# The order of ScalarE's work in one outer-layer step, and one pass for x plus normed x

## The reference, cut to what matters

```
xn   = layernorm(x)                                   # 6250 x 256
agg  = [sum, max, mean of the edge rows by target node]       # 3 x 96
x1   = x + (relu([xn, agg, u0] @ W1 + b1) @ W2 + b2 + xn)     # hidden 1024
x2   = layernorm(x1)
out  = x1 + layernorm(x2 + top2_of_16_experts(x2)) * gamma + beta
```

## Time and profile before

| | us |
|---|---|
| median of 3 runs (1345.76 to 1350.47) | 1348.34 |
| the profiled execution's own time | 1347.68 |
| its span, first to last instruction | 1346.0 |
| PE busy | 1187.7 (88%) |
| DVE busy | 785.8 (58%) |
| POOL busy | 777.8 (58%) |
| ACT busy | 646.7 (48%) |

### The profile page before, as it was taken

The page is one execution under the profiler, slowest core; times in us unless marked ns, Lnnn a source line. Parts: engine busy times, 40 slices in busy tenths (PEclk is TensorE's granted clock), DMA queues, the critical chain, the costliest instruction groups (busy, mean ns, idle before and its releaser), DMA issues.

```text
span 1346.0 us, 28248 instructions
## 1 busy us (share of the span) xinstructions
PE 1187.7 (88%) x6684; PEld 1003.9 (75%) x6685; DVE 785.8 (58%) x3039; ACT 646.7 (48%) x1969; POOL 777.8 (58%) x1061
## 2 busy tenths in 40 slices
PE   2003899999988999999999999999999999999798
PEld 1002688887877878878888888999999999997333
DVE  5999999799899799800454203552222222222887
ACT  5962465664565656647654442222332333333454
POOL 4875566665665656666675335656666666663222
PEclk7555899998989989999999999999999999998555
DMA  9986576777758754791111248855665666663762
GB/s 318 294 250 250 222 261 242 280 282 284 282 210 309 250 204 169 271 308 43 45 54 36 77 161 266 304 180 205 210 212 195 213 209 209 215 209 124 250 204 92
DMA packets 113876, 282.66 MB, mean 210 GB/s; under 512 B 23697, under 2 KB 36371, under 8 KB 113669
## 3 DMA queue, kind: packets, MB, share of 16 engines
q1 hardware_dynamic: 76785, 218.39, 46.9%
q0 software_dynamic: 26048, 43.47, 10.4%
q10 hardware_dynamic: 10964, 19.96, 4.3%
HBM read 167.27 MB, written 114.25 MB: 209 GB/s over the span
## 4 chain that ended last, share of the span: by engine, by line
PE 59%; DVE 16%; issue 7%; DMA 7%; POOL 5%; ACT 4%; POOLq 1%; ACTq 1%; SPq 0%; DVEq 0%
PE ps L1158 15%; PE ps L1166 14%; PE ps L1048 7%; DVE mem L1253 6%; DVE mem L1257 6%; PE ps L1034 5%; PE ps L1036 5%; DMA mem<-piece_carry,mem 4%; PE ps L1199 3%; PE ps L1201 3%; PE ps L1144 2%; POOL mem L571 1%; POOL mem L572 1%; PE ps L1084 1%; DMA mem<-in_edge_attr_dram 1%
## 5 line engine op out<-in xcount | busy, mean ns | idle before, releaser
L924 ACT ACTIVATE mem<-ps,mem 128x128 f32<-128x128 f32 x452 | 129.3, 368 | 301.7 <-PE ps L1158 270.3
L1034 PE MATMUL ps<-mem 128*128 128x250 f32 x800 | 213.1, 390 | 25.1 <-ACT mem L826 23.6
L1158 PEld LDWEIGHTS ps<-mem 128*128 128x128 f32 x1808 | 218.0, 192 | 8.8 <-issue 3.2
L1158 PE MATMUL ps<-mem 128*128 128x128 f32 x1808 | 221.1, 276 | 1.4 <-issue 1.4
L1166 PE MATMUL ps<-mem 128*128 x904 | 214.3, 380 | 2.6 <-issue 2.2
L1253 DVE TENSOR_TENSOR_SCAN mem<-ps,mem 128x80 f32<-128x80 f32 x960 | 207.9, 307 | 0.3
L1257 DVE TENSOR_TENSOR_SCAN mem<-ps,mem 128x80 f32<-128x80 f32 x960 | 207.9, 319 | 0.0
L1036 PE MATMUL ps<-mem 128*128 128x250 f32 x800 | 207.5, 383 | 0.0
L1034 PEld LDWEIGHTS ps<-mem 128*128 128x128 f32 x800 | 155.8, 198 | 45.7 <-ACT mem L826 25.5
L664 POOL DMA_INDIRECT expert_rows<-mem x113 | 113.7, 1006 | 123.1 <-DVE mem L1515 78.8
L1048 PE MATMUL ps<-mem 128*125 128x256 f32 x800 | 181.0, 379 | 0.7 <-ACT mem L826 0.7
(11 more groups left out here) (252 smaller groups left out, 1696.2 us busy)
## 6 DMA issues: line engine op xcount, KB each, us to landing
mem<-in_L_ffn_w_dram SPq DMA_DIRECT2D x129, 512.0 KB
run_sum<-mem SPq DMA_DIRECT2D x40, 960.0 KB
run_max<-mem SPq DMA_DIRECT2D x40, 960.0 KB, 7.2
mem<-in_edge_attr_dram SPq DMA_DIRECT2D x36, 960.0 KB
mem<-expert_rows SPq DMA_DIRECT2D x22, 512.0 KB, 5.4
x_rows<-mem ACTq DMA_DIRECT2D x25, 256.0 KB, 2.1
x_normed<-mem ACTq DMA_DIRECT2D x25, 256.0 KB
mem<-in_x_dram ACTq DMA_DIRECT2D x24, 256.0 KB
```

Of the source, the lines that this page charges most:

```text
L924: ins = act.activation(hT[b][:, c, :], bank(2 + b, c * P, (c + 1) * P), ACT.Relu, bias=eb1c[:, bass.ds(e, 1), c])
L1034: pe.matmul(h, W1x[:, c, hc * P:(hc + 1) * P], XT[b][:, c, :], start=(c == 0), stop=False)
L1158: ins = pe.matmul(bank(2 + b, f * P, (f + 1) * P), w1now[q][:, c, f * P:(f + 1) * P], XgT[b][:, c, :], start=(c == 0), stop=(c == DC - 1))
```

## The change

- In ScalarE's list `relu(i, 0)` moves ahead of `carry_in`.
- The two GpSimd passes L617 and L619 become one: ScalarE computes x + xn directly, as x times (rstd + 1) plus shift, in two activations (`twice`), placed between the moments of x1 and `mask_rows`. GpSimd then adds only b2, and does so at the end of its step, behind `gather`, instead of right behind `add_rows`. `norm1` gets one more tiny operation (rstd + 1), and its results get two buffers.
- The load of x for block i+2 moves from ahead of `mask_rows` to behind `relu(i, 1)`.
- TensorE transposes x2 of block i-1 behind layer 2 instead of between its halves; ScalarE copies it out (`take_x2`) behind `take_g` instead of ahead of it.

```
@@ norm1 (GpSimd)
-                s2.mark(pool.tensor_tensor(rstd_1, dev_1, rpow, ALU.pow))
+                s2.mark(pool.tensor_tensor(rstd_1[:, b], dev_1, rpow, ALU.pow))
                 s2.wait()
-                pool.tensor_tensor(nmr_1, mean1, rstd_1, ALU.mult).then_inc(rstd1_ready, 1)
+                pool.tensor_tensor(shift_1[:, b], mean1, rstd_1[:, b], ALU.mult)
+                pool.tensor_scalar(twice_1[:, b], rstd_1[:, b], 1.0, None, ALU.add).then_inc(rstd1_ready, 1)
@@ residual (GpSimd)
-                pool.tensor_tensor(RES, XN[b], XR[b][0:NT], ALU.add).then_inc(residual_ready, 1)
-                pool.wait_ge(residual_ready, 2 * i + 1)
+            def residual(i):
+                pool.wait_ge(twice_rows, i + 1)
                 pool.tensor_tensor(RES, RES, b2bc, ALU.add).then_inc(residual_ready, 1)
@@ rows_step (GpSimd)
                     add_rows(i - 1)
-                residual(i, g, b)
...
                     gather(*after(i, g, b, 2))
+                residual(i)
@@ new function (ScalarE)
+            def twice(i, b):
+                if not isinstance(i, int) or i:
+                    act.wait_ge(x1_ready, i)
+                for a in range(2):
+                    ins = act.activation(RES[:, a, :], XR[b][0:NT, a, :], ACT.Identity, bias=shift_1[:, b, a:a + 1], scale=twice_1[:, b, a:a + 1])
+                ins.then_inc(twice_rows, 1)
@@ gnn_step (ScalarE)
                     moments1(*after(i, g, b), 1)
+                relu(i, 0)
+                if more:
                     carry_in(*after(i, g, b))
-                relu(i, 0)
...
                     moments2(i - 1, 1)
-                if not isinstance(i, int) or i + 2 < MACROS:
-                    act.wait_ge(residual_ready, 2 * i + 2)
-                    load_x(i + 2, b)
+                twice(i, b)
                 if more:
                     mask_rows(*after(i, g, b))
                 relu(i, 1)
+                if not isinstance(i, int) or i + 2 < MACROS:
+                    act.wait_ge(twice_rows, i + 1)
+                    load_x(i + 2, b)
...
                     store_x2(i - 1, to)
+                take_g(i, g, b)
+                if norm:
                     take_x2(i - 1)
-                take_g(i, g, b)
@@ gnn_step (TensorE)
-                layer2(i, g, b, between2)
+                layer2(i, g, b, amid2)
+                if not isinstance(i, int) or i >= 1:
+                    turn_x2(i - 1)
```

More of the change, by code:

```diff
@@ L222, in gnn_moe_kernel @@
         rowU = k.take(TILES, parts=NT, dt=U32)
-        mean1, dev_1, rstd_1, nmr_1 = (k.take(2, parts=NT) for _ in range(4))
+        mean1, dev_1 = (k.take(2, parts=NT) for _ in range(2))
+        rstd_1, twice_1, shift_1 = (k.take(2, 2, parts=NT) for _ in range(3))
         Lo = k.take(TILES, NX, parts=NT)
@@ L369, in gnn_moe_kernel @@
         xr_got = [sem(f"xr_got{i}") for i in range(2)]
-        residual_ready, x1_ready = sem("residual_ready"), sem("x1_ready")
+        twice_rows, residual_ready, x1_ready = sem("x_and_normed_x"), sem("residual_ready"), sem("x1_ready")
         moments2_step, norm2_step, rstd2_ready = sem("moments2_step"), sem("norm2_step"), sem("norm2_rstd_ready")
@@ L586, in join, with norm1 @@
                 pool.tensor_tensor(RAW[b][:, :, 1, :], take_c, take_p, ALU.add).then_inc(joined, 1)
-            def norm1(i):
+            def norm1(i, b):
                 s2 = Steps(pool, norm1_step, i * 2)
@@ L592, in norm1 @@
                 s2.wait()
-                s2.mark(pool.tensor_tensor(rstd_1, dev_1, rpow, ALU.pow))
+                s2.mark(pool.tensor_tensor(rstd_1[:, b], dev_1, rpow, ALU.pow))
                 s2.wait()
-                pool.tensor_tensor(nmr_1, mean1, rstd_1, ALU.mult).then_inc(rstd1_ready, 1)
+                pool.tensor_tensor(shift_1[:, b], mean1, rstd_1[:, b], ALU.mult)
+                pool.tensor_scalar(twice_1[:, b], rstd_1[:, b], 1.0, None, ALU.add).then_inc(rstd1_ready, 1)
             def add_rows(i):
                 pool.wait_ge(g_out, i + 2)
-                pool.wait_ge(residual_ready, 2 * i + 2)
+                pool.wait_ge(residual_ready, i + 1)
                 pool.tensor_tensor(GO, GO, RES, ALU.add).then_inc(x1_ready, 1)
@@ L625, in rows_step @@
                     add_rows(i - 1)
-                residual(i, g, b)
                 if more:
                     cut(*after(i, g, b))
-                    norm1(i + 1)
+                    norm1(i + 1, 1 - b)
                     join(*after(i, g, b))
@@ L634, in rows_step @@
                     gather(*after(i, g, b, 2))
+                residual(i)
             pool.sem_inc(joined, 1)
             gather(0, 0, 0)
-            norm1(0)
+            norm1(0, 0)
             cut(0, 0, 0)
@@ L811, in mask_rows @@
                 for a in range(2):
-                    ins = act.activation(XN[b][:, a, :], XR[b][0:NT, a, :], ACT.Identity, bias=nmr_1[:, a:a + 1], scale=rstd_1[:, a:a + 1])
+                    ins = act.activation(XN[b][:, a, :], XR[b][0:NT, a, :], ACT.Identity, bias=shift_1[:, b, a:a + 1], scale=rstd_1[:, b, a:a + 1])
                 ins.then_inc(node_rows, 1)
+            def twice(i, b):
[4 more added lines that the diff above has]
+                ins.then_inc(twice_rows, 1)
             def take_turned(i, g, b):
@@ L1093, in between1 @@
                         amid1()
[L1095 to L1099, removed]
                 layer1(i, g, b, between1)
```

## The result

The changed kernel takes 1356.79 us (median of 5, 1352.21 to 1360.14), the kernel before 1349.03 us (5 runs beside them, 1345.76 to 1350.47). The ratio is 1.0058 with a 95% interval of 1.0032 to 1.0085: 0.6% slower. The forecast was 1354, 2.8 us short of that. It stood on a median of 1348.34 for the kernel before, from three runs; as a difference to the kernel before, 5.7 us were forecast and 7.8 measured. The profiled execution of after is its slowest, 1360.14 us with a span of 1358.4, 3.35 above its median. Its rows are read with that in mind.

A forecast was written before the change was run, and what follows sets the result against it. PE was taken as the bound, with only its outer-layer holes, about 35 us, to win. Terms -5.4, +2.0, +3 +3, +2, 0 and +1.0 gave +5.6 us, so 1354 us, 0.4% slower; range 1340 to 1376.

The forecast's parts named there:

- ScalarE's stretch: ScalarE's list from the relu to the end of `mask_rows`: 9.66 us, so normed x is complete 17.36 us into the step.
- The hand-over: From normed x complete on ScalarE to PE's first transpose: 0.26 us.
- the hole: PE idle ahead of `turn` in every step: 1.66 us, bounds 1.4 and 1.9.
- Steps 1 to 19: Outer-layer steps: 19 x 26.08 = 495.5 us against 493.55, +2.0; late gathers and their clock +3 +3.
- late gathers: Gathered rows landing after 8 us or more lengthen the new hole: 3 us in all, and 3 us for clock falls.
- Step 0: First outer-layer step: `turn` at 144.4 + 0.26 instead of 150.06, -5.4 us.
- Steps 22 and 23: Late outer-layer steps: long PE work ahead of `turn` hides the hole, 0.
- Steps 20 and 21: Outer-layer steps with extra router work of DVE and PE, partly hiding the hole: +2 us.
- rival D: GpSimd's and ScalarE's ring, 0.5 us short of binding, becomes the bound: 0.3 to 0.7 us a step, 1360 to 1367; chance 0.10.
- rival B: The new hole also costs clock: +18 us, 1372, if half the steps fall at 1.8 us; 1390 if all; chance 0.20.
- x2 at the end: Transposes and copy of x2 exposed behind the last step, ahead of the router matmuls: PE loses about 1.0 us.
- Rival C: Not slower, the hole ahead of `turn` absent or much smaller: 1347 under 1.3 us, 1318 without any hole; chance 0.22.

The follow-up runs named there:

- e3: The changed kernel with `twice` moved behind the second relu, out of the stretch ahead of `mask_rows`: 1357.00 us, ratio 1.0061 to the kernel before.
- e4: The kernel before with two edits, relu(i, 0) ahead of carry_in and the load of x behind relu(i, 1): 1341.61 us, ratio 0.9951.
- e1: The kernel before with one edit, relu(i, 0) ahead of carry_in on ScalarE: 1351.23 us, ratio 1.0014.
- e7: As e4, and `mask_rows` hands over normed x before the aggregates, each with its own semaphore: 1329.81 us, ratio 0.9866 to the kernel before.
- e8: The changed kernel with one extra activation of 125x256 into an unused tile ahead of normed x: 1374.38 us, one run.
- e10: The changed kernel with two extra activations of 125x256 into unused tiles ahead of normed x: 1380.56 us, one run.
- e11: The changed kernel with one extra activation of 125x64 into an unused tile ahead of normed x: 1377.10 us, one run.
- e9: As e7, with the gather issued in two halves, the residual's passes behind `join` and their wait ahead of `norm1`: 1316.46 us, ratio 0.9771 to the kernel before.
- e2: The changed kernel with relu(i, 0) put back behind carry_in: 1355.07 us, ratio 1.0048 to the kernel before.
- e5: The changed kernel with x2 turned between the halves of layer 2 and `take_x2` ahead of `take_g`, as before: 1351.39 us, ratio 1.0032 to the kernel before.
- e6: The kernel before with the late turn of x2 alone: 1350.16 us, ratio 1.0014.

## Why the prediction was right, and where a term was off

**ScalarE's stretch decides the step: right.** Predicted: normed x at 17.36 us, measured 17.34. The terms hold one by one in step 18: relu, carried sums and logits 1.50 + 1.96 = 3.46 predicted, 611.88 - 608.41 = 3.47 measured; moments of x1 2.37 and 614.22 - 611.88 = 2.34; `twice` 0.98 and 615.21 - 614.22 = 0.99; `mask_rows` 2.85 and 618.04 - 615.21 = 2.83; in all 9.66 and 9.63. The hand-over was 0.05 and not 0.26: the 0.26 of the earlier trace rows was read at the first transposes of the program and came in no later step. So PE's transposes start 1.45 us later than before (17.39 us into the step against 15.94) after an idle time of 1.36, where I had 1.66 for both, and the step is 25.85, not 26.08. That is 4.4 us over 19 steps, at the lower bound that I gave for the hole (1.4). e3 and e4 add one thing that my sum did not hold: without `twice`, GpSimd's `join` would have been the next to bind, 0.29 us behind the moments, so `twice` costs 0.73 us a step and not its full 0.99.

**Steps 1 to 19: +8.0 predicted, +7.38 measured, by two errors that cancel.** The undisturbed part is 19 x 25.85 = 491.15, 2.4 us under before, where I had +2.0. The rest is 500.93 - 491.15 = 9.8 us where I had 6: 8.7 in the three steps with late gathers and their falls of the clock, 1.1 in small delays of other steps. That the sum fits so well is luck. In e1, e4 and e7 this rest was 16 to 17 us. In a shorter step the carried sums come sooner after the same issues, and the kernels with the longest steps bear this out (at most one late step each in e8, e10 and e11). But e1's step is only 0.11 us shorter than that of the changed kernel, and it had six late steps where the latter had three: the length alone doesn't set it, and what else does stays open. It is the term that I sized worst in every forecast. Only e9, which issues earlier, ends it at steps of 24.4 us.

**Step 0: -5.4 predicted, -5.84 measured. Steps 22 and 23: 0 and 0. Steps 20 and 21: +2 predicted, +3.46 measured**, since the router work hid none of the hole there: both steps have a hole of 1.50 us, and the relu starts 0.38 and 0.14 us later than before.

**The ring (rival D): the 0.5 us to spare was about right.** I had `add_rows` at 2.8 us and the end of the moments of x at 7.2; in steps 15 and 17 of the changed kernel they are at 3.5 and 7.8, in most others lower, and in steps 1 to 19 the relu starts at 7.99 at the latest. e3 shows that the ring binds once the stretch is 0.7 us shorter. By the code, the moments wait for `add_rows` only because the store of x1 stands ahead of them in ScalarE's list; moving it was not tried. The load of x was issued 16.1 to 16.7 us into the step, not at 19, and the moments never waited for it.

**The clock (rival B): did not come, but was near.** Behind 1.35 to 1.52 us the clock stayed at 1.00 in all undisturbed steps, and behind 2.33 in step 3; behind 3.12 and 3.21 it was 0.50. Reading a point between 0.75 and 2.11 us off was the weak part: e2 has falls behind 0.85 us and e4 none behind 2.79. The argument against B, that PE was dense ahead of the new hole while the router's matmuls stood before the old one, fits e2's falls; the two places were not otherwise compared.

At 1.70 us, 0.34 more and 0.04 above my own value for the hole, e11 shows 11 of 19 steps with a fall at 1.68 us each, 18.5 us: rival B at its price of +18. The Trainium skill, page "TensorE: Matmul & The Clock Gate", section "A second HAM failure mode: psum-queue depth-cycling", says that short holes which come back are enough; the runs agree for 1.70 us and more ahead of `turn` and for 0.85 in e2, and not for 1.35 to 1.52 in the changed kernel.

**x2 at the end: +1.0 predicted, +0.91 measured on the way to the experts; a missing term behind it.** The expert tiles took 6.6 us more in this profile, though no line of theirs was changed. Over the profiles, the seven kernels with the late turn took 438.65 to 446.2 us there (mean 443.6), the six with the turn in the middle (before, e1, e4, e5, e7, e9) 436.5 to 441.3 (mean 438.7). In after, the clock was down at the tiles' start (5.44 us for the first 32 matmuls) and gathered rows came 3.43 us late.

But six of those seven have `twice` and the later b2 pass as well. The only kernel with the late turn alone is e6, 438.65 us, and the only one with `twice` and the turn in the middle is e5, 437.85: both lie among the others. So a cost of some 5 us in the tiles is seen only where both come together, in one profile of each kernel; in medians it is the 3.5 us between e5 and the changed kernel, with intervals that overlap. The clock does not explain it: e9 has the fall at the tiles' start (5.44) without the late turn, at 439.46. What does stays open.

My sum had the tiles unchanged. In the profiles its terms add up to 5.9 us (-5.84 + 7.38 + 3.46 + 0.91) where I had 5.6; the expert tiles' 6.6 are what makes the profiled execution 12.4 longer. Of the 2.8 us by which 1354 was low in medians, 0.7 is the median of the kernel before, and the tiles can hold the rest.

**Which part costs.** In ratios to the kernel before, adding one part after the other: the swap 1.0014 (e1), with the load of x out of the stretch 0.9951 (e4), with `twice` and the later b2 pass 1.0032 (e5), with the late turn of x2 1.0058 (the changed kernel). In steps with nothing late: the swap alone on the kernel before 25.74, and 25.2 and 25.3 in steps 1 and 18 (e1), with the load of x out of the stretch 25.12 (e4, 0.5% faster than before), with `twice` in it 25.85 (after). `twice` puts 0.99 us on the one engine that had none to give, to free 1.1 us of GpSimd; with x2 late, it turns a change that was worth 7 us into one that costs 8. GpSimd's freed pass by itself was not tried.

**Two slips in the working.** Rival C's time without any hole, 1318, doesn't follow from the 35 us beside it, which give 1348 - 35 = 1313. Two falls of the clock at 1.8 us are 3.6 us, not 3. Neither changes the forecast by more than 0.6 us.

## What to carry to other kernels

When a wait is removed, add up the list of the engine that feeds the next hand-over, instruction by instruction, from a row to a row: here that gave the new hole to 0.3 us. Then look at what becomes the bound next (here a ring through GpSimd, and the landing of gathers): in e3 the two took back nearly all that the shorter stretch won, and in e4 the late gathers cost 10 us more than expected. The gain came from handing over first what the consumer can start on (e7) and from issuing long transfers in parts as early as their inputs allow (e9). In this kernel a hole that comes back in every step cost nothing beyond its length at 1.4 us, and about 1 us a step more at 1.7.

## What the runs showed that I had not expected

The clock behind a returning hole follows a pattern and not one length at which it falls: no fall at 1.35 to 1.52 us, two of three steps at 1.70 (up to step 14), about every other one at 1.85, every third at 2.35, each fall costing 1.4 to 1.7 us. The longer hole thus had fewer falls, so the hole's length alone doesn't decide; the length of the step differs too (25.85 to 26.83), and the two were not varied apart. One run of each kernel with a profile carries this. The holes that late rows made in the other kernels say the same: ahead of `turn` there were falls behind 2.08 us (e1) and 2.10 (e5) and none behind 2.62 (e1) and 2.79 (e4); ahead of the second half there were falls behind 0.85 and 1.16 (e2) and none behind 1.97 (e6). All 19 holes over 2.8 us in steps 1 to 19 of the profiles had a fall behind them.

The rows of a gather landed about 8 us after its last issue in the late steps of before; over a whole run, e4, it was 2.4 to 9.9. In e7 six of 19 steps were late, in e9 none. e9 issues half of the gathers some 16 us earlier and the last one about 3 us earlier, and moves the residual's passes; the profile counts the same 113876 DMA packets in both. Together this was worth 13 us; how much of it each move gave was not told apart.
